# A two-layer pair-interaction kernel: 78 pairs of the seventh K-tile are dealt out anew, 34 of them into one rounded pass

## What is computed

```python
def _cin_layer(x0, xk, W, b):
    out = jnp.einsum('bhd,bmd,shm->bsd', xk, x0, W) + b[None, :, None]
    return jax.nn.relu(out)
x1 = _cin_layer(x0, x0, W1, b1)     # x0: B=1024, M=39, D=16; W1: 128x39x39
x2 = _cin_layer(x0, x1, W2, b2)     # W2: 128x128x39
p1 = x1.sum(axis=-1); p2 = x2.sum(axis=-1)
h = jnp.concatenate([p1, p2, dense_ctx], axis=1)
h = jnp.maximum(h @ W_top1 + b_top1, 0.0)
h = jnp.maximum(h @ W_top2 + b_top2, 0.0)
y = h @ W_top3
```

## Time and profile before

| | us |
|---|---|
| median of 3 runs (1188.96 to 1189.38) | 1189.1 |
| the profiled execution | 1195.75 |
| its span, first to last instruction | 1193.7 |
| PE busy in the span | 1110.4 |
| DVE busy | 946.2 |
| POOL busy | 842.8 |
| ACT busy | 801.2 |

### The profile page before, as it was taken

One profiled execution on the slowest core, in us unless ns is written; L12 is line 12 of the kernel. 1 busy time (PEld: TensorE's weight loads), 2 busy tenths in 40 slices (PEclk: granted clock), 3 DMA queues, 4 the chain that ended last, 5 costly groups with the idle time before them and its releaser, 6 DMA issues.

```text
span 1193.7 us, 17611 instructions
## 1 busy us (share of the span) xinstructions
PE 1110.4 (93%) x4507; PEld 830.7 (70%) x4507; DVE 946.2 (79%) x2860; ACT 801.2 (67%) x2718; POOL 842.8 (71%) x951
## 2 busy tenths in 40 slices
PE   0059999999999999999999999999999999999998
PEld 0027777777777777777777667777777777777687
DVE  4027888889898989898888668888888888886787
ACT  5016767777777767777777567777677777775674
POOL 6754787788687887788688646887877884453354
PEclk9999999999999999999999999999999999999999
DMA  6256568764876568674876428765676757763342
GB/s 178 37 125 141 110 126 174 153 137 88 178 165 125 117 131 184 135 149 87 183 163 124 98 49 180 164 134 106 130 176 144 147 97 175 168 130 78 66 86 48
DMA packets 73708, 154.70 MB, mean 130 GB/s; under 512 B 14435, under 2 KB 27637, under 8 KB 73606
## 3 DMA queue, kind: packets, MB, share of 16 engines
q0 software_dynamic: 28272, 85.81, 40.6%
q1 hardware_dynamic: 45334, 67.77, 21.4%
HBM read 66.49 MB, written 3.81 MB: 59 GB/s over the span
## 4 chain that ended last, share of the span: by engine, by line
PE 81%; DVE 6%; issue 5%; DMA 2%; ACT 2%; SPq 2%; another core or an unknown queue 1%; DVEq 0%; ACTq 0%
PE bank L682 63%; PE l_acc L666 15%; DVE acc L548 3%; DMA z<-e_rows 2%; ACT prod L421 1%; PE misc L715 1%; PE misc L711 1%; DVE z L508 1%; DVE p2acc L566 0%; DMA e_rows<-e_t 0%; DVE t_sum L556 0%; DVE p L589 0%; DVE t_sum L560 0%; DVE p2l L602 0%
## 5 line engine op out<-in xcount | busy, mean ns | idle before, releaser
L421 ACT ACTIVATE prod<-bank,emb 128x128 f32<-128x128 f32 x2552 | 720.5, 376 | 305.5 <-PE bank L682 272.4
L548 DVE SCALAR_TENSOR_TENSOR acc<-bank,emb,acc 128x128 f32<-128x128 f32 x2184 | 613.3, 340 | 142.7 <-PE bank L682 124.7
L682 PE MATMUL bank<-w2h,x1h 128*128 128x512 f32 (+1 forms) x1280 | 535.4, 418 | 9.4 <-DVE acc L548 6.1
L682 PE MATMUL bank<-w2l,x1h 128*128 128x512 f32 (+1 forms) x1280 | 494.3, 386 | 0.0
L682 PE MATMUL bank<-w2h,x1l 128*128 128x512 f32 (+1 forms) x1280 | 467.0, 427 | 5.5 <-issue 3.8
L310 POOL DMA_INDIRECT emb<-tbl,idx x312 | 310.5, 995 | 82.2 <-issue 76.0
L682 PEld LDWEIGHTS bank<-w2h,x1h 128*128 128x128 f32 x1280 | 240.8, 188 | 107.6 <-issue 56.9
L682 PEld LDWEIGHTS bank<-w2h,x1l 128*128 128x128 f32 x1280 | 240.5, 188 | 89.8 <-issue 35.7
L330 POOL TENSOR_TENSOR tree<-prod 128x640 f32<-128x640 f32 x127 | 240.2, 1892 | 83.2 <-DMA prod<-prod 83.2
L682 PEld LDWEIGHTS bank<-w2l,x1h 128*128 128x128 f32 x1280 | 240.7, 188 | 61.5 <-issue 22.4
L321 POOL DMA_DIRECT2D prod<-prod x127 | 125.1, 985 | 173.7 <-ACT prod L421 171.5
(11 more groups left out here) (96 smaller groups left out, 289.3 us busy)
## 6 DMA issues: line engine op xcount, KB each, us to landing
prod<-prod POOLq DMA_DIRECT2D x127, 640.0 KB
z<-e_rows SPq DMA_DIRECT2D x160, 234.0 KB
z<-e_rows SPq DMA_DIRECT2D x192, 78.0 KB
emb<-tbl,idx POOLq DMA_INDIRECT x312
z<-e_rows SPq DMA_DIRECT2D x32, 156.0 KB
prod<-w_by_h SPq DMA_DIRECT2D x3, 832.0 KB
e_rows<-e_t SPq DMA_DIRECT2D x8, 256.0 KB
wt<-w_top SPq DMA_DIRECT2D x2, 512.0 KB
```

The source lines that it names most:

```text
L421: last = nc.scalar.activation(prod[:, ct % P_RING, i, n * S:(n + 1) * S], bank[:, (ct * NB + k) % RING, n * S:(n + 1) * S], ACT.Copy, scal ...
L548: nc.vector.scalar_tensor_tensor(dst, src, scale, dst if step else b2_row[:, :], ALU.mult, ALU.add).then_inc(v_step, 1)
L682: last = nc.tensor.matmul(out_bank[:, 0:b - a], x, w[:, a:b], start=(n == 0), stop=(n == 2))
```

## The change

The seventh K-tile is dissolved. Its shifts 18 and 19 had 78 pairs. 44 of them (11 to a tile) go into partitions 117 to 127 of K-tiles 1 to 4, which now fill 128 rows. The other 34 form a new K-tile `REST`: each pair stands in three rows, 102 in all, and the table `marks` turns the three copies into (high weight, high product), (high weight, low product) and (low weight, high product), so that one pass in rounded float32 gives nearly the full product. The weights of it (`w_rest`) are prepared once at the start.

For the products DVE makes the 102 rows like another K-tile; ACT rounds them into `rest` (`round_rest`), and DVE mixes high and low (`mix_rest`), both new, once a chunk. The first operand of the 34 pairs is loaded by four new transfers of SP into `rest` (`load_rest_first`), issued ahead of the next chunk's `load_shifted`; the second operand by four more inside it. In three chunks of four ACT copies the first operand to the PSUM bank `e_rep` at g = 38 of the chunk before (`copy_first`); DVE makes `REST` first, and then ACT copies the usual rows to the same bank at g = 4 instead of g = 26. In a tile's first chunk (`direct`) DVE reads `rest` in SBUF, and `e_rep` is copied at g = 26 as before. `load_shifted` and `load_rest_first` together move 1078 rows of 2 KB a chunk.

The transposes and their copies come six positions sooner (`LIFT_AT` 4, 9 for 10, 15), and the gathers up to two `ct` sooner. `y` moves into `h2`, so ACT waits for an earlier output's transfer a step sooner in the top network.

The diff, cut to its core:

```diff
-Z_GROUPS = (range(0, 1), range(1, 4), range(4, 7))
 NF = 7
+REST = NF - 1
+Z_GROUPS = (range(0, 1), range(1, 4), range(4, REST))
 NK = M // 2 + 1
-F_ROWS = [M * min(KP, NK - KP * t) for t in range(NF)]
+EXTRA = P - KP * M
+EXTRA_TILES = 4
+REST_RANGES = ((18, 11, 21), (18, 32, 39), (19, 11, 20), (19, 31, 39))
+N_REST = sum(b - a for _, a, b in REST_RANGES)
+F_ROWS = [P] * EXTRA_TILES + [KP * M] * (REST - EXTRA_TILES) + [3 * N_REST]
...
-MAKE_AT = (1, 4, 7, 10, 13, 16, 19)
-CONTRACT_AT = (7, 10, 13, 16, 19, 22, 25)
+MAKE_AT = (2, 5, 8, 11, 14, 16, 19)
+FIRST_AT = 38
+SWAP_AT = 4
 X1_AT = 27
 X1L_AT = 31
 P1_AT = 34
 P1_FOLD_AT = 38
-LIFT_AT = (10, 15)
-LIFT_COPY_AT = (12, 17)
+LIFT_AT = (4, 9)
+LIFT_COPY_AT = (6, 11)
...
+def direct(f):
+
+    return f % CPT == 0
+
+
+def make_order(f):
+    if f == 0:
+        return tuple(range(NF))
+    return (0, 1, REST, 2, 3, 4, 5) if direct(f) else (REST, 0, 1, 2, 3, 4, 5)
+
+
+def made_before(f, t):
+
+    return make_order(f).index(t)
+
+
+def contractions(f):
+
+    if f == 0:
+        return dict(zip((7, 10, 13, 16, 19, 22, 25), range(NF)))
+    if direct(f):
+        return {9: 0, 12: 1, 17: 2, 20: 3, 21: REST, 22: 4, 25: 5}
+    return {11: 0, 14: 1, 17: 2, 18: REST, 20: 3, 22: 4, 25: 5}
+
+
+def round_at(f):
+    return 20 if f == 0 else 11 if direct(f) else 6
+
+
+def mix_at(f):
+    return 21 if f == 0 else 15 if direct(f) else 12
...
+def pairs(t):
+
+    if t == REST:
+        rest = [(h, (h + k) % M) for k, a, b in REST_RANGES for h in range(a, b)]
+        return [(3 * i + c, h, m) for c in range(3) for i, (h, m) in enumerate(rest)]
+    rows = [(k * M + h, h, (h + KP * t + k) % M) for k in range(KP) for h in range(M)]
+    if t < EXTRA_TILES:
+        rows += [(KP * M + h, h, (h + KP * REST + t) % M) for h in range(EXTRA)]
+    return rows
...
+def rest_marks():
+
+    marks = np.zeros((P, 3), np.float32)
+    for c, values in enumerate(((0, 1, 0), (1, -1, 0), (0, -1, -1))):
+        marks[c:3 * N_REST:3] = values
+    return marks
...
-            return min((TILES - 1) * M, -(-M * (ct + 9) // 16))
+            return min((TILES - 1) * M, -(-M * (ct + 9 + min(2, ct // 4)) // 16))
...
+            def rest_rows(f, row, n):
+                tile, q = divmod(f, CPT)
+                return bass.AP(tensor=e_rows[tile % 2], offset=row * ROW + q * CH, ap=[[ROW, n], [0, 3], [1, CH]])
+
+            def load_rest_first(f):
+                sp.wait_ge(et_stored[f // CPT % 2], 64 * (f // CPT // 2 + 1))
+                wait(sp, f_used, NF * f)
+                at = 0
+                for _, a, b in REST_RANGES:
+                    sp.dma_start(rest[3 * at:3 * (at + b - a), :].bitcast(F32), rest_rows(f, a, b - a)
+                                 ).then_inc(in_first, 16)
+                    at += b - a
...
+                sp.dma_start(z[KP * M:P, r, NF, :], rows(0, [[ROW, EXTRA], [1, CH]])).then_inc(in_rep[r], 16)
...
             for f in range(CHUNKS):
+                if f > 1:
+                    load_rest_first(f - 1)
                 if f % CPT == 0:
                     store_rows(f // CPT)
                 load_shifted(f)
+                if f == 0:
+                    load_rest_first(0)
                 if f == BATCH_IN[0] + 5:
                     store(0)
+            load_rest_first(CHUNKS - 1)
             store(1)
...
             def copy_rep(f):
-                act.wait_ge(in_rep[f % 2], 48 * (f // 2 + 1))
-                wait(act, f_made, NF * f)
-                nc.scalar.copy(e_rep[0:KP * M, :], z[0:KP * M, f % 2, NF, :]).then_inc(rep_ready, 1)
+                act.wait_ge(in_rep[f % 2], 64 * (f // 2 + 1))
+                wait(act, f_made, NF * f if direct(f) else NF * f + 1)
+                nc.scalar.copy(e_rep[:, :], z[:, f % 2, NF, :]).then_inc(rep_ready, 1)
+
+            def copy_first(f):
+                act.wait_ge(in_first, 64 * (f + 1))
+                act.wait_ge(f_made, NF * f)
+                nc.scalar.copy(e_rep[0:3 * N_REST, :], rest[0:3 * N_REST, :].bitcast(F32)).then_inc(first_ready, 1)
+
+            def round_rest(f):
+                act.wait_ge(f_made, NF * f + made_before(f, REST) + 1)
+                nc.scalar.copy(rest[0:3 * N_REST, :], z[0:3 * N_REST, f % 2, REST, :]).then_inc(rest_high, 1)
...
+                    if f < CHUNKS and g == round_at(f):
+                        round_rest(f)
...
                         copy_lifted(c // CPT + 1, LIFT_COPY_AT.index(g))
-                    if f + 1 < CHUNKS and g == REP_AT:
+                    if f < CHUNKS and g == SWAP_AT and not direct(f):
+                        copy_rep(f)
+                    if f + 1 < CHUNKS and g == REP_AT and direct(f + 1):
                         copy_rep(f + 1)
+                    if f + 1 < CHUNKS and g == FIRST_AT and not direct(f + 1):
+                        copy_first(f + 1)
                     if c in BATCH_IN:
                         if g == SPLIT_AT[0]:
                             round_p1(BATCH_IN.index(c))
...
+                part = z[0:rows, f % 2, t, :]
+                if t == REST:
+                    dve.wait_ge(in_second[f % 2], 64 * (f // 2 + 1))
+                    if direct(f):
+                        dve.wait_ge(in_first, 64 * (f + 1))
+                        first = rest[0:rows, :].bitcast(F32)
+                    else:
+                        dve.wait_ge(first_ready, f - f // CPT)
+                        first = e_rep[0:rows, :]
+                    nc.vector.tensor_tensor(part, first, part, ALU.mult).then_inc(f_made, 1)
+                    return
                 dve.wait_ge(rep_ready, f + 1)
                 for k, ts in enumerate(Z_GROUPS):
                     if t == ts[0]:
-                        dve.wait_ge(in_z[f % 2][k], 48 * (f // 2 + 1))
-                nc.vector.tensor_tensor(z[0:rows, f % 2, t, :], e_rep[0:rows, :], z[0:rows, f % 2, t, :], ALU.mult
-                                        ).then_inc(f_made, 1)
+                        dve.wait_ge(in_z[f % 2][k], Z_LOADS[k] * (f // 2 + 1))
+                nc.vector.tensor_tensor(part, e_rep[0:rows, :], part, ALU.mult).then_inc(f_made, 1)
+
+            def mix_rest(f):
+                rows = F_ROWS[REST]
+                dve.wait_ge(rest_high, f + 1)
+                nc.vector.scalar_tensor_tensor(rest[0:rows, :], z[0:rows, f % 2, REST, :], marks[0:rows, 0:1],
+                                               rest[0:rows, :].bitcast(F32), ALU.mult, ALU.subtract
+                                               ).then_inc(rest_mixed, 1)
 
...
-            def contract(f, t):
+            def contract(f, turn, t):
                 rows = F_ROWS[t]
-                pe.wait_ge(f_made, NF * f + t + 1)
-                if t == 0:
+                if turn == 0:
                     pe.wait_ge(w1_summed, 1)
                     wait(pe, l1_free, f)
                     wait(pe, x1l_done, f)
-                nc.tensor.matmul(l1_acc[:, :], w1[0:rows, t, :], z[0:rows, f % 2, t, :],
-                                 start=(t == 0), stop=(t == NF - 1)).then_inc(f_used, 1)
+                if t == REST:
+                    pe.wait_ge(w_rest_mixed, 1)
+                    pe.wait_ge(rest_mixed, f + 1)
+                    w, x = w_rest[0:rows, :], rest[0:rows, :]
+                else:
+                    pe.wait_ge(f_made, NF * f + made_before(f, t) + 1)
+                    w, x = w1[0:rows, t, :], z[0:rows, f % 2, t, :]
+                nc.tensor.matmul(l1_acc[:, :], w, x, start=(turn == 0), stop=(turn == NF - 1)).then_inc(f_used, 1)
 
             def layer2_bank(c, j, k):
                 ct = c * DC + j
```

More of the change, by code:

```diff
@@ L84, in pair_weights @@
     for t in range(NF):
[L85 to L91 removed]
+        for p, h, m in pairs(t):
+            ahead[p, t] = w1[:, h, m]
+            if m != h:
+                back[p, t] = w1[:, m, h]
+    return ahead, back
+def rest_marks():
[3 more added lines that the diff above has]
+    return marks
 def build(nc, dram, tables, out):
@@ L123, in build @@
         z = sb("z", [P, 2, NF + 1, CH])
+        rest = sb("rest", [P, CH], F32R)
+        w_rest = sb("w_rest", [P, S], F32R)
         x1h = sb("x1h", [P, 2, CH], F32R)
@@ L379, in _ @@
             nc.scalar.copy(back_stage, w1_back).then_inc(back_staged, 1)
+            act.wait_ge(in_marks, 16)
+            act.wait_ge(w1_summed, 1)
+            nc.scalar.activation(w_rest[:, :], w1[:, REST, :], ACT.Copy, scale=marks[:, 1:2]).then_inc(w_rest_high, 1)
             for k, (a, b) in enumerate(W2_PIECES):
@@ L798 @@
         "ids": load("ids", inputs["ids"]),
+        "marks": load("rest_marks", rest_marks()),
         "ident": load("ident_const", np.eye(P, dtype=np.float32)),
```

58 lines of the change are left out of this document (36 added, 22 removed).

## The result

The changed kernel takes 1178.2 us (median of 4 executions, 1174.2 to 1183.1), the kernel before beside it 1189.0: a ratio of 0.9923, 95% interval 0.990 to 0.9946. I had forecast 1175.1 and a range of 1166.5 to 1185. The profiled execution of after is its slowest, 1183.1 with a span of 1181.2; that of before had a span of 1193.7.

A forecast was written before the change was run, and what follows sets the result against it. The prediction took PE to bound the kernel. Its terms, -20.2 - 4.3 + 5 + 4 + 1.5, summed to -14.0 us, which from the median of 1189.1 gave 1175.1, with a range of 1166.5 to 1185.

The forecast's parts named there:

- PE's work: In each of 32 chunks one float32 contraction of 0.86 gives way to a rounded pass of 0.23: -20.2 us.
- Sooner transposes: In seven chunks with transposes, ACT's copy to `e_rep` no longer waits for `z`: -4.3 us (-2.5 to -4.3).
- The prologue: ACT's copy of chunk 1's first operand waits for `rest` ahead of the first scaling: +5 us (2 to 9).
- DVE and ACT: New copies, roundings and mixes in the chunks are mostly hidden, but mixes may be held long: +1.5 us (0 to 4).
- the lock: A VectorE instruction with two SBUF inputs and a GpSimd one reading SBUF exclude each other; counted within the +1.5 us.
- POOL late: POOL's sum comes late for DVE's merge, first in chunks 1 to 4: +4 us (1 to 12).
- all is covered: Rival: the prologue costs 2, POOL 1, the locks nothing, giving 1167.6 us; chance 0.15.
- POOL is late in every tile: Rival: longer adding transfers use up POOL's freedom, losing 1.6 us a tile, 10 in all: 1181 to 1187; chance 0.13.
- slower: Rival: larger `z` loads delay POOL's adding transfers until POOL paces the kernel, 1209 us; chance 0.06 shared with the next rival.
- The pass is not cheap: Rival: the rounded pass costs PE 0.86, so nothing is gained there, about 1195 us; chance 0.06 shared with "slower".

The follow-up runs named there:

- rest_f32: The changed kernel with the new pass on `rest` run in full float32: 1208.8 us, 1.0098 of the kernel before.
- before_lift: The kernel before with only the transposes and their copies six positions sooner: 1182.9 us, 0.9969 of the kernel before.
- late_lift: The changed kernel with the transposes and their copies back at the old positions: 1197.2 us, 1.0002 of the kernel before.
- combo: `close_next` with chunk 1's first operand read directly from `rest` and ACT's copy of its rows behind chunk 0's rounding: 1159.1 us, 0.9765 of the kernel before.
- close_next: The changed kernel with the merge's closing step moved into the next chunk, tile sum and top network later: 1169.0 us, 0.9853 of the kernel before.
- chunk1_direct: The changed kernel with chunk 1 treated like a tile's first chunk, without ACT's early wait for `rest`: 1184.4 us, 0.9898 of the kernel before.
- combo_gathers: `combo` with the gathers back where they were before the change: 1181.2 us, 0.987 of the kernel before.
- after2: The changed kernel measured again, unaltered, on another chip: 1181.1 us, 0.9951 of the kernel before.
- combo_no_mix: `combo_gathers` without DVE's mix of high and low products, the pass reading the rounded product: 1180.6 us, 0.9862 of the kernel before.
- old_gathers: The changed kernel with the gathers back where they were before: 1193.0 us, 0.996 of the kernel before.
- tsum_psum: The changed kernel with the merge's tile `t_sum` in PSUM instead of SBUF in most chunks: 1188.6 us, 0.9929 of the kernel before.
- more_rows: `combo_gathers` with a further unused load of 351 rows in every chunk: 1205.6 us, 1.008 of the kernel before.
- first and third group: Two sets of four experiment kernels, each set sharing a chip, where the kernel before took 1197.3 and 1197.8 us.

## Why the prediction came out as it did

The forecast was -14.0. Measured were -10.9 on the first chip and -5.8 on the second, both inside the range, and both smaller than forecast. That the first came within 3.1 us of the sum is in part luck: the prologue's term was 5 too small.

**PE's work, -20.2: right.** Undisturbed chunks are 0.67 shorter, the pass shows 0.23 in the chain, and `rest_f32` gives 0.65 a chunk back, 20.8 us of PE's work.

**Sooner transposes, -4.3: right, measured alone** at -4.0 in `before_lift`. Six positions were enough, as forecast. For the changed kernel the trace of `late_lift` doesn't confirm that the wait would come back.

**The prologue, +5 (2 to 9): mechanism right, size too small.** ACT waits for `rest` ahead of its first scaling, at 86.40, inside the 80 to 95 that I had named:

```profile
86.40 0.59 ACT L504 COPY e_rep<-rest 102x512 f32<-102x512 f32 x1 [9.46 <-DMA rest<-e_rows]
```

Taking the wait away is worth 10.0 us (`combo` against `close_next`, 8.1 of it at the start of chunk 1). On chips with slower issues chunk 1 starts 9 us sooner (`chunk1_direct`) or only 4.2 (`combo_gathers`). The step that failed is "without that standstill the load would be through by about 79, and the new wait costs 2 to 3". SP in `after2`, without a standstill:

```profile
78.64 3.93 SPq L364 DMA_DIRECT2D z<-e_rows  x4
82.69 3.06 SPq L337 DMA_DIRECT2D rest<-e_rows  x4
```

The four transfers are issued from 82.7 on, behind chunk 1's whole load. I should have counted the new instructions in SP's queue: 19 transfers for chunk 1 where there were 12, and the four behind them. The two profiles hide this term, because the one of before had its odd standstill at the same place: chunk 1 starts at 120.3 before and 118.4 after, as if nothing had been added. In that profile SP's issues are slow, first row, as they are not in `before_lift`, second row:

```profile
57.20 10.97 SPq L278 DMA_DIRECT2D z<-e_rows  x9
57.35 5.57 SPq L278 DMA_DIRECT2D z<-e_rows  x9
```

That the slow issues make the standstill is likely, not shown. The clean prologue of the kernel before is the 110.0 of `before_lift`.

**DVE and ACT, +1.5 (0 to 4): the lock is real, the place was wrong, and it was too small.** I had looked for it at the new mix, which costs 0.6 where it was measured (`combo_no_mix`). It strikes at the merge, an old part of the kernel. Of what the earlier trace rows said, I used only that such instructions can be long, not that this very line is one of them and that DVE has little to spare behind it: from the end of a bank's scaling to the matmul that needs the bank there are 2.0 to 3.5 us at positions 11 to 21 of an undisturbed chunk of after, and only 0.05 to 1.3 at 29 to 39, behind the closing step.

Why it costs more now than before is not shown. It isn't that less is left to spare behind the closing step: in chunk 27 of before and of after the room at positions 29 to 39 is the same to 0.01 us (1.26, 0.98, 0.71, 0.28, 0.63, 1.21). What differs is how often a closing step of 2.6 us or more follows a first step of 3.6 or more: never in the profile of before, once in `before_lift`, three times in after (and 4.07 us in its last chunk), twice in `old_gathers`, once each in `after2`, `late_lift`, `chunk1_direct` and `rest_f32`. The Trainium skill ("SBUF — State Buffer", the section on SBUF's two separate sides) says that a VectorE operation in a two-port fast mode and a GpSimd operation exclude each other for their whole length, and so does one with two SBUF inputs where the GpSimd operation reads SBUF. Here `tsum_psum` agrees on both forms of the closing step. The form with two inputs reached 4072 ns and with one of them in PSUM 681; L694, 405 ns from SBUF and 680 from PSUM, was held 2.67 us in the first and never in the second. The Trainium skill's page also says that whichever starts first gets the ports. The rows of chunk 3 above don't show that: DVE's instruction begins at 205.81, 1.1 us ahead of POOL's addition, and ends behind it, at 209.45.

**POOL late, +4 (1 to 12): it happens, later and less.** DVE waited 0.2 us for POOL's sum in after and 2.9 in `after2`, not in chunks 1 to 4, but in `late_lift`, `tsum_psum` and `combo` the first of these waits lie in chunk 3. Chunks 7 and 15 of `after2`, each with a wait of 1.2, are 1.1 us over. The 0.2 us that I had read as such a wait in the kernel before lies at 647 us, not at 380, and the profile names no engine as its cause; no row there shows the merge held by POOL. `combo_gathers` shows that the waits come without the shifted gathers, though `old_gathers` has none. The adding transfers did get longer with 20% more rows, by 1.4 us in the median, inside my 0 to 1.5 (from issue to landing, last number; `before_lift`, then after):

```profile
prod<-prod POOLq DMA_DIRECT2D x127, 640.0 KB, 5.5
prod<-prod POOLq DMA_DIRECT2D x127, 640.0 KB, 6.9
```

But POOL waited less for them (67.4 for 83.2 us), so the term I drew from it was wrong for this size; with a third more rows the waiting grew.

Put together on the second chip: -20.2 - 4.0 + 10.0 is -14.2, and the measured difference is -5.8. The 8.4 between is about what `close_next` wins beyond the 3.9 us of the sums over a tile, 12.1 - 3.9 = 8.2. That it agrees so well is partly luck, and it doesn't show that the change brought the 8.4. The kernel before has such collisions too, one in the profile of `before_lift` (chunk 4, 35.75 long), and with the closing step moved it might gain as much; that run is missing. The profiles show less than 8.4: chunks 1 to 31 take 1014.4 in `after2` and 1030.7 in `before_lift`, 16.3 less, where 30 chunks of 0.67 would be 20.1. That leaves 3.8, partly POOL's lateness, though the profiled execution of `after2` is the fastest of its twelve. On the first chip the difference was -10.9; the two intervals, 0.990 to 0.9946 and 0.9937 to 0.9965, hardly overlap, and why isn't known. Executions of the changed kernel lie 8 us apart (1178.1 to 1186.1, twelve in `after2`), those of `close_next` and `combo` 4 (five each), but those of the kernel before lie 8 apart as well, so what spreads them stays open.

The rivals: "all is covered" fell with the prologue. "POOL is late in every tile" and "slower" didn't come, but `more_rows` shows that the second wasn't far. "The pass is not cheap" was priced by `rest_f32` at a ratio of 1.0098, slower than the kernel before.

## What to carry to other kernels

When a change takes work from the bounding engine, list what the engine next to it has to spare at every position, not its busy share; here much was lost in a step that the change never touched, and moving that step by 23 positions, with the sum that follows it, was worth 12.1 us on a chip where the change was worth 5.8. Try such a move on the old kernel too, or you can't say what the change has to do with it. An instruction with two SBUF inputs beside a busy POOL should be costed at its longest row, not its median, or have one input in PSUM. In a prologue, count every transfer that a new wait stands behind in its queue, and take a second profile before you trust a first one with a standstill in it.

## What was not expected of the hardware

- Issuing is of two speeds in the prologue. In `after2` SP issued the second and third group of three `z` transfers, at 59.83 and 61.48, in 1.20 and 2.52 us; in `old_gathers`, on another chip, the same two took:

```profile
64.62 2.79 SPq L357 DMA_DIRECT2D z<-e_rows  x3
...
69.51 4.90 SPq L357 DMA_DIRECT2D z<-e_rows  x3
```

 There the first bank starts at 89.0 instead of 78.2, and the kernel before takes 1197 instead of 1187. All eight profiles of the first and third group are of the slow kind, and so is that of before in the earlier trace rows. What slows it wasn't looked into.

- A stall of PE was followed by a lower clock, once. In the last chunk of after the closing step took 4.07 us, and PE waited 2.81 us for DVE. The stretch behind it, by windows (us, busy times by engine, granted clock, DMA share, GB/s), had

```profile
1162.40:1166.30 3.90, 3.85 (x10) 3.07 (x11) 3.90 (x16) 0.00 (x0) 2.42 (x4) 0.56 0.00 0
1166.40:1170.00 3.60, 3.60 (x30) 3.36 (x28) 3.50 (x12) 0.00 (x0) 0.00 (x0) 1.00 0.00 0
```

 a granted clock of 0.56, near the lower of TensorE's two levels, 1.2 GHz: passes of 512 columns stood 0.43 apart instead of 0.23. This tail is 4.7 us longer than that of `after2`. No other stall of after behind chunk 0 was as long; behind the one of 1.63 us in chunk 3 the granted clock was 1.00.
